# Another order of the layers' slots, of the layers' end and of the last tile's down rows

## The reference

```python
# block 1: 64 features (DIM), 4 layers, inner width 256
h = x @ Win.T + bin
for each layer:
    y = silu(layernorm(h, l1w, l1b))
    y = sconv(y)          # y[t] = Re(sum over s<=t of p**(t-s) y[s] + last * p**(t+1))
    h = h + y * scl
    y = layernorm(h, l2w, l2b)
    h = h + silu(y @ W1.T + b1) @ W2.T + b2
x = norm(x + layernorm(h, lnl_w, lnl_b) @ Wout.T + bout)
# block 2: weights are looked up in a codebook of 8192 rows of 8 numbers
Wg, Wu, Wd = codebook[idx_gate], codebook[idx_up], codebook[idx_down]   # 1376x512, 1376x512, 512x1376
x = norm(x + (silu(x @ Wg.T) * (x @ Wu.T)) @ Wd.T)
```

## Time and profile before

| | |
|---|---|
| median of three runs | 1266.31 us |
| the profiled execution, its own time | 1264.5 us |
| its span, first to last instruction | 1262.5 us |
| PE busy | 1188.8 us (94%) |
| DVE busy | 1011.6 us (80%) |
| POOL busy | 929.9 us (74%) |
| ACT busy | 261.7 us (21%) |
| mean granted clock of PE | 0.982 of full speed |

### The profile page before, as it was taken

How to read it: one execution, slowest core, us unless ns; L and a number is a source line. 1 busy time by engine, 2 the same in 40 slices (tenths; PEclk the granted TensorE clock), 3 DMA queues, 4 the chain that set the end, 5 groups by cost and what they waited for, 6 DMA issues and landing times.

```text
span 1262.5 us, 16835 instructions
## 1 busy us (share of the span) xinstructions
PE 1188.8 (94%) x5595; PEld 839.3 (66%) x5595; DVE 1011.6 (80%) x2194; ACT 261.7 (21%) x395; POOL 929.9 (74%) x895
## 2 busy tenths in 40 slices
PE   6857998889999999999999999999999999999998
PEld 4533444346777777777777777777777777778876
DVE  3998898878997778888777888778888778888845
ACT  2325777772000000000000000000000000000024
POOL 6777777777777777777777777777777777777710
PEclk8968999989999999999999999999999999999999
DMA  9331211102433223433223433333433333334303
GB/s 202 64 68 37 45 37 39 27 4 53 105 92 87 65 71 80 95 82 92 65 69 79 89 85 81 65 70 86 93 85 87 67 70 79 94 72 88 60 2 133
DMA packets 96971, 93.57 MB, mean 74 GB/s; under 512 B 53549, under 2 KB 57909, under 8 KB 96886
## 3 DMA queue, kind: packets, MB, share of 16 engines
q1 hardware_dynamic: 64692, 83.86, 23.0%
q0 software_dynamic: 28160, 3.66, 8.5%
q10 hardware_dynamic: 4034, 4.98, 1.4%
HBM read 87.53 MB, written 4.90 MB: 73 GB/s over the span
## 4 chain that ended last, share of the span: by engine, by line
POOL 73%; issue 21%; PE 4%; DMA 1%; DVE 0%; ACT 0%; POOLq 0%; SPq 0%; DVEq 0%
POOL stage_down L400 57%; POOL stage_up L389 16%; PE bank L652 2%; PE cand L652 2%; DMA work<-in_L_ffn_idx_up 0%; DMA stage_down<-in_L_ffn_codebook,idx_down 0%; ACT x L505 0%; POOLq L160 0%; DVE chosen L1229 0%; DVE x L1033 0%; PE bank L924 0%; SPq L315 0%; DVE idx_low L1091 0%; DVE idx_low L1092 0%; DVE shift L1239 0%
## 5 line engine op out<-in xcount | busy, mean ns | idle before, releaser
L400 POOL DMA_INDIRECT stage_down<-in_L_ffn_codebook,idx_down x688 | 722.3, 1050 | 209.7 <-issue 209.1
L652 PE MATMUL cand<-one_hot,book 128*128 128x512 f32 (+1 forms) x2432 | 622.7, 398 | 19.0 <-DVE one_hot L1057 19.0
L1057 DVE TENSOR_SCALAR one_hot<-bc,low_of 128x512 fp32r<-128x512 uint16 (+1 forms) x1216 | 512.8, 482 | 99.0 <-PE cand L652 97.3
L652 PEld LDWEIGHTS cand<-one_hot,book 128*128 128x128 f32 x2432 | 449.7, 189 | 187.2 <-DVE one_hot L1057 51.8
L389 POOL DMA_INDIRECT stage_up<-in_L_ffn_codebook,idx_up x192 | 205.6, 1071 | 63.8 <-issue 58.2
L652 PE MATMUL bank<-x1t_hi,w 128*128 128x512 f32 (+1 forms) x704 | 239.1, 396 | 0.0
L1075 DVE SCALAR_TENSOR_TENSOR chosen<-bc,high_of,cand 128x512 f32<-128x512 uint16 (+1 forms) x304 | 220.2, 724 | 21.1 <-PE bank L652 17.9
L652 PEld LDWEIGHTS bank<-x1t_hi,w 128*128 128x128 f32 (+1 forms) x704 | 130.3, 185 | 31.4 <-issue 2.1
L652 PE MATMUL bank<-x1t_lo,w 128*128 128x512 f32 (+1 forms) x352 | 137.7, 391 | 0.0
L598 ACT ACTIVATE prod<-bank 128x512 f32<-128x512 f32 (+1 forms) x44 | 26.3, 599 | 389.4 <-PE bank L652 389.4
L605 ACT ACTIVATE act_hi<-prod 128x512 fp32r<-128x512 f32 x40 | 25.3, 633 | 342.5 <-DVE prod L1033 342.5
(11 more groups left out here) (181 smaller groups left out, 751.8 us busy)
## 6 DMA issues: line engine op xcount, KB each, us to landing
bc<-index_parts SPq DMA_DIRECT2D x272, 256.0 KB, 3.3
stage_down<-in_L_ffn_codebook,idx_down POOLq DMA_INDIRECT x688, 2.7
bc<-index_parts_rest SPq DMA_DIRECT2D x32, 192.0 KB, 3.1
x<-in_L_attn_x ACTq DMA_DIRECT2D x4, 1024.0 KB, 9.8
out_x<-x SPq DMA_DIRECT2D x16, 256.0 KB, 2.0
stage_up<-in_L_ffn_codebook,idx_up POOLq DMA_INDIRECT x192
index_parts<-parts_t SPq DMA_DIRECT2D x20, 32.0 KB, 2.0
w_in<-in_L_attn_W ACTq DMA_DIRECT2D x2, 256.0 KB
```

The lines of the kernel that those rows point to most:

```text
L400: pool.indirect_dma_start(stage_down[k % RING][:, q, j * CS:(j + 1) * CS], None, a["L0_ffn_codebook"], bass.IndirectOffsetOnAxis(ap=idx_do ...
L652: return pe.matmul(dst, lhs, rhs, start=start, stop=stop)
L1057: done = v.tensor_scalar(one_hot[quad % 2][:, q, 0:nw], bc[quad % BCS][:, 0:nw], low_of[:, q:q + 1], None, ALU.is_equal)
```

## The change

In the slots, PE's `mixed(t - 1)` moves from ahead of `variance1(t)` to behind `spread(t - 2)`; DVE's `add_mixed(t - 1)` moves from the slot's start to behind `choose` of the first quad, and `add_back` ahead of `norm2`; ACT's `silus` moves ahead of `square2`. The damped d gets a second buffer. In the layers' end, ACT makes roots together and silus together, so that one pair of table loads falls away, and PE's and DVE's steps are put in an order that suits it. In the tail, the last tile's down rows are turned after chunk 1 instead of chunk 0, and with them `down` and `out_chunk` come one chunk later; another two table loads fall away there.

```diff
-            work = at("work", [P, 13, C])
+            work = at("work", [P, 14, C])
+        d = [work[:, n, :] for n in (6, 13)]
@@ ACT, slot t
+                if t >= 2:
+                    silus(t - 2)
                 if t:
                     square2(t - 1)
-                if t >= 2:
-                    silus(t - 2)
                 square1(t + 1)
@@ ACT, layers' end
+            def tile_root(n):
+                act.wait_ge(s["aggregated"], n + 1)
+                root(rstd[:, n:n + 1], mv[:, n, 1:2]).then_inc(s["rstd_made"], 1)
             square2(ITEMS - 1)
+            root2(ITEMS - 1)
+            tile_root(0)
             silus(ITEMS - 2)
+            silus(ITEMS - 1)
             square1(ITEMS + 1)
-            root1(ITEMS + 1)
-            root2(ITEMS - 1)
-            for n in range(NT + 2):
+            for n in range(1, NT + 2):
                 if n == 2:
-                    silus(ITEMS - 1)
                     square1(ITEMS + 2)
+                if n == 3:
+                    root1(ITEMS + 2)
...
+                if n == 1:
+                    root1(ITEMS + 1)
@@ PE
             def mixed(i):
                 pe.wait_ge(s["damped"], i + 1)
-                if i >= 3:
-                    pe.wait_ge(s["h_made"], i - 2)
-                mm(bank[0][:, :], mix[:, i // NC, :], d).then_inc(s["mixed"], 1)
+                if i:
+                    pe.wait_ge(s["h_mid"], i)
+                if i >= 2:
+                    pe.wait_ge(s["h_made"], min(ITEMS - NC + 1, i - 1))
+                mm(bank[0][:, :], mix[:, i // NC, :], d[i % 2]).then_inc(s["mixed"], 1)
...
-                if t:
-                    mixed(t - 1)
                 variance1(t)
...
                 if t >= 2:
                     spread(t - 2)
+                if t:
+                    mixed(t - 1)
@@ PE, layers' end
             back(ITEMS - 3)
+            variance2(ITEMS - 1)
             project(0)
             spread(ITEMS - 2)
             project(1)
+            spread(ITEMS - 1)
+            back(ITEMS - 2)
             variance1(ITEMS + 1)
-            variance2(ITEMS - 1)
-            back(ITEMS - 2)
@@ PE, tail
-            for c in range(NC + 1):
+            for c in range(NC + 2):
                 if c < NC:
                     hidden(FULL, REST, c, 0, 1)
-                if c == 0:
+                if c == 1:
                     turn_down(FULL, REST)
-                else:
-                    for t in range((c - 1) * TPC, c * TPC):
+                if c >= 2:
+                    for t in range((c - 2) * TPC, (c - 1) * TPC):
@@ DVE, slot t
-                if t:
-                    add_mixed(t - 1)
                 one_hots(quads[0] + 1)
...
+                if t >= 3:
+                    add_back(t - 3)
                 if t >= 2:
                     norm2(t - 2)
-                if t >= 3:
-                    add_back(t - 3)
...
+                if t >= 2:
+                    v.wait_ge(s["mixed"], t - 1)
+                tt(d[t % 2], g, tab[:, l, :], ALU.mult).then_inc(s["damped"], 1)
+                choose(quads[0])
                 if t:
-                    v.wait_ge(s["mixed"], t)
-                tt(d, g, tab[:, l, :], ALU.mult).then_inc(s["damped"], 1)
-                choose(quads[0])
+                    add_mixed(t - 1)
```

More of the change, by code:

```diff
@@ L235, in build @@
             centre = at("centre", [P, P])
-        sq1, rs1, xn, y, u, g, d = (work[:, n, :] for n in range(7))
+        sq1, rs1, xn, y, u, g = (work[:, n, :] for n in range(6))
+        d = [work[:, n, :] for n in (6, 13)]
         sq2 = [work[:, 7 + b, :] for b in range(2)]
@@ L566, in _ @@
             square2(ITEMS - 1)
+            root2(ITEMS - 1)
+            tile_root(0)
             silus(ITEMS - 2)
+            silus(ITEMS - 1)
             square1(ITEMS + 1)
-            root1(ITEMS + 1)
-            root2(ITEMS - 1)
-            for n in range(NT + 2):
+            for n in range(1, NT + 2):
                 if n == 2:
-                    silus(ITEMS - 1)
                     square1(ITEMS + 2)
+                if n == 3:
+                    root1(ITEMS + 2)
                 if n == 4:
-                    root1(ITEMS + 2)
-                if n == 5:
                     square1(ITEMS + 3)
-                if n == 7:
+                if n == 6:
                     root1(ITEMS + 3)
@@ L584, in _ @@
                     normalize(n - 1, n, "x1_made")
+                if n == 1:
+                    root1(ITEMS + 1)
                 if n < NT:
-                    act.wait_ge(s["aggregated"], n + 1)
-                    root(rstd[:, n:n + 1], mv[:, n, 1:2]).then_inc(s["rstd_made"], 1)
+                    tile_root(n)
             def down_hi(k, n):
@@ L638, in _ @@
                 product_hi(FULL, REST, c)
-                if c == 0:
+                if c == 1:
                     down_hi(FULL, REST)
-                if c >= 2:
-                    out_chunk(c - 2)
+                if c >= 3:
+                    out_chunk(c - 3)
+            out_chunk(NC - 3)
             out_chunk(NC - 2)
@@ L866, in variance2 @@
                     pe.wait_ge(s["state_kept"], t // NC * (NC - 1) + t % NC)
-                if i:
+                if i == ITEMS - 1:
+                    pe.wait_ge(s["rs2_made"], i)
+                elif i:
                     pe.wait_ge(s["ff_made"], i)
@@ L872, in back @@
                 pe.wait_ge(s["ff_made"], i + 1)
-                pe.wait_ge(s["h_mid"], min(ITEMS, i + 3))
+                pe.wait_ge(s["h_mid"], i + 2 if i < ITEMS - 3 else ITEMS)
                 if i:
@@ L881, in spread @@
                 pe.wait_ge(s["normed2"], i + 1)
-                pe.wait_ge(s["rs1_made"], min(ITEMS + 2, i + 3))
-                pe.wait_ge(s["rs2_made"], i + 1)
+                if i == ITEMS - 1:
+                    pe.wait_ge(s["ff_made"], i)
+                pe.wait_ge(s["rs1_made"], min(ITEMS + 1, i + 3))
+                pe.wait_ge(s["rs2_made"], i + 1 if i < ITEMS - 2 else ITEMS)
                 for k in range(FK):
@@ L958, in _ @@
             project(1)
+            spread(ITEMS - 1)
+            back(ITEMS - 2)
             variance1(ITEMS + 1)
-            variance2(ITEMS - 1)
-            back(ITEMS - 2)
             for n in range(1, NT + 1):
+                if n == 2:
+                    back(ITEMS - 1)
                 if n == 3:
                     variance1(ITEMS + 2)
-                    back(ITEMS - 1)
-                if n == 6:
+                if n == 5:
                     variance1(ITEMS + 3)
@@ L969, in _ @@
                     project(n + 1)
-                if n == 1:
-                    spread(ITEMS - 1)
                 if n in AHEAD_STEPS:
@@ L1325, in _ @@
                     norm2(ITEMS - 1)
+                if n == 2:
                     add_back(ITEMS - 2)
-                if n == 2:
                     norm_last(1)
-                if n == 4:
+                if n == 3:
                     add_back(ITEMS - 1)
@@ L1401, in _ @@
                     product_lo(FULL, REST, c)
-                if c == 0:
+                if c == 1:
                     down_lo(FULL, REST)
+                if c >= 3:
+                    make_shift((c - 3) * TPC, TPC, NT + c - 2)
                 if c >= 2:
-                    make_shift((c - 2) * TPC, TPC, NT + c - 1)
-                if c:
-                    for t in range((c - 1) * TPC, c * TPC):
+                    for t in range((c - 2) * TPC, (c - 1) * TPC):
                         add_down(last_pair, t, (bank[2][:, :], cand[0][:, :], cand[1][:, :], cand[2][:, :]))
```

6 lines of the change are left out of this document (3 added, 3 removed).

## The result

The changed kernel takes 1297.04 us, the median of four runs (1294.10 to 1299.75), against 1266.82 for the kernel before: a ratio of 1.0245, 95% interval 1.0208 to 1.0283. It is slower, as forecast, but by 30 us where the sum said 18: inside the range of 8 in 10 (1268 to 1300) and outside the forecast's own (1277 to 1292). The profiled execution took 1294.88 us, its span is 1293.1 and PE's mean granted clock 0.969 instead of 0.982. One of the ten executions of f2_end_warm, a kernel further down, took 2626 us, and its ratio leaves that one out.

What follows compares the result with a forecast made beforehand. PE bounds the main stage, a cycle of waits the slots before it; 12.3 + 2 + 3 + 1 - 0.3 = +18.0 us on the profiled 1264.5 gives 1282.5, forecast 1284 us against the median, own range 1277 to 1292, 8 in 10: 1268 to 1300.

Steps and rivals of the forecast that it cites:

- square2's 1.4 us: Sign, slots: square2's wait for DVE's h addition, about 1.4 us each, becomes ACT's largest wait there.
- root1(16): Sign, start of the layers' end: this root comes 14 to 18 us later than before.
- 240 to 291: Sign, stretch of the layers' end ahead of the main stage: keeps its length within 4 us.
- Cycle of the slot: Slots 4 to 15: cycle of waits grows from 8.71 to 9.92 us, +12.3 us in all with two-group slots and picks.
- Slots 0 to 3: First four slots: 41 us instead of 38.9, +2 (0 to +4).
- PE's clock in the slots: Slots: PE's pauses of about 2.7 us drop its clock; four slots of 0.8, +3 us (bounds 0 and +10).
- the fall at 116: Earlier trace: PE busy 1.36 of 3.6 us up to 116.0, then granted clock 0.50 at 118 to 120.
- Layers' end: End of the layers: one pair of table loads saved, new waits; -1 at 2.4 GHz, about +4 at 1.2 GHz, taken +1 us.
- Tail: Last tile: PE's 0.34 us wait for the last gather goes, -0.3 us.
- Addition not last: Rival, slots: add_mixed done before silus ends, cycle 8.44 us, total 1256 us; chance 0.08.
- Hidden: Rival: longer cycle right, but early, two-group and last slots give back as much, about 1266 us; chance 0.08.
- The clock's rival: Every slot's pause drops PE to 1.2 GHz, 17.6 us instead of 3, end +4: 1302 us; chance 0.12.

Runs made afterwards that it cites:

- f2_end_warm: Changed kernel with slots in the order of before, new end and tail kept, 18 extra matmuls in the end's pauses: 1267.7 us.
- e2: Changed kernel with its layers' end put back into the order of before, new slots and tail kept: 1293.2 us.
- e5: Changed kernel with add_mixed ahead of choose on DVE, nothing else, on the slower chip: ratio 1.0061 to 1.0104 to the kernel before.
- f1_three: Changed kernel with norm2 ahead of add_back, add_mixed ahead of choose and square1 ahead of square2; new end and tail kept: 1273.4 us.
- e3: Changed kernel with norm2 ahead of add_back again on DVE, nothing else: 1294.9 us.
- e1: Changed kernel with the slots of all three engines in their order of before; new end and tail kept: 1271.8 us.
- e11: f1_three with the layers' end of before as well: 1272.4 us.

## Why the prediction was right, and where it was too small

Of its signs, the period, square2's 1.4 us, the vanished wait for mixed, PE's pause and the length of the main stage came. Three did not: root1(16) came 23.7 us later and not 14 to 18, 240 to 291 grew by 7.4 us and not by at most 4, and ACT's largest wait was silus'.

- **Cycle of the slot: right.** 9.92 forecast; 9.91 and 9.93 measured, square2's wait 1.37 (1.4 forecast), PE's pause 2.83 (2.7). Twelve slots at full clock come to about 123 (e2's slope) or 13.2 us more than before (the full slots' mean), against 122.3 and +12.3. e5 and f1_three show the cause: with add_mixed ahead of choose the slot is 9.26 us, and with square1 ahead of square2 as well (and norm2 ahead of add_back) 8.74, as forecast from the same steps. Twelve slots at 9.92 were not seen in one run: slots 13 and 14, at 1.00 and 0.99, took 10.55 and 10.51.
- **Slots 0 to 3: right**, +2.3 against +2.
- **PE's clock in the slots: mechanism right, size wrong.** "I take four slots of 0.8, +3" measured 8.8, near the upper bound of 10. Six of twelve slots had a fall, 1.5 us each and not 0.8. Two things were missed. A slow back, variances and spread follow each other in the slot, so the slot pays more than one of them; and add_back ahead of norm2, which the sum costed at nothing, puts norm2 behind the slow back as well (some 4 of the 8.8, by e3's one profile). The row chosen against the bound, 0.54 of 2 us busy at 144 to 146 with the clock left at 1.00, was from a kernel whose slots pause less. The Trainium skill ("TensorE: Matmul & The Clock Gate", section "HAM oscillation — how this bites in real kernels") says that repeated pauses throttle the clock again and again; the slots here agree with it (0.92 against 1.00), though PE's pauses, 3.2 us at most, are shorter than those of the page's example. It and the fall at 116 together should have weighed more than that one row.
- **Layers' end: the step that failed.** "+1", with a bound of +4; measured +7.4. Up to tile 4 it is +3.6: the walk was right for 2.4 GHz (22.42 in f2 against 22.9), but its "-1" set this against a 23.7 of before that was measured at 0.86. At that clock the new order is 2.3 us longer (f1, and 2.4 in e1), and a longer fall (0.81) adds 1.3. Why it is longer is argued and not shown: tile 0's normalisation now stands behind silus(15), and silus(15) waits 4.89 us for spread(15) and back(14). No run has the first part of before's end at full clock, so its "-1" can't be told. And "From tile 4 on both go by DVE's 2 us a tile" was wrong at 1.2 GHz, where PE sets this part: 31.95 at 0.79 instead of 28.17, +3.8. After, the addition for tile 6 waits, PE and then DVE:

```profile
294.88 2.07 PE L659 MATMUL cand<-woutt,work 65*128 65x512 f32 x2
```

```profile
296.99 0.69 DVE L1046 TENSOR_TENSOR x<-x,cand 128x512 f32<-128x512 f32 x1 [2.47 <-PE cand L659]
```

  The projection takes 2.07 us behind a variance of 2.07 (each 1.12 at full clock), and DVE is idle for 2.47. The saved table loads are real (ACT's busy time in the end falls from 37.97 to 35.76 us); the end is longer all the same.
- **Tail: right as far as can be told**, -0.5 for main stage and tail against -0.3, from one profile of before. The gap of the earlier trace rows is gone: `turn_down`'s first row has no idle before it. POOL waited 20.2 us once for PE's unit, and it cost nothing, as PE is later still.

```profile
POOL stage_up L390 <- PE bank L659: 23.1, 2, 20.2
```

- **Rivals.** "Addition not last" and "Hidden" did not come. The clock's rival (17.6 in the slots, end +4: 1302) is half true, and the measured 1297 lies nearer to it than to the forecast's 1284. 8.8 in the slots and 5.1 of the 7.4 in the end go with a lower clock than before, and the other 2.3 are the new order at before's clock. Together they are 16 us where the sum had 4, which is nearly the whole miss of 12 us. That the direction was right owes nothing to luck, as the cycle alone gives 13 of the 30 us; that the time fell into the wide range owes something to it.

What stays open is what makes a fall come in one execution and not in the next of the same instructions.

## What to carry to other kernels

Where several engines hand work round in a cycle, price the exchange of two neighbours by who waits behind the later one: here an addition behind four steps of DVE, with two squares, a table load and the roots queued behind it, made each slot 1.2 us longer, and three exchanges of neighbours gave back 24 us, falls of the clock included. A change that lengthens PE's pauses must be priced at both clocks for every later step, those that another engine seems to set included, and the measured part of before that it is compared with must be read with its clock. Filling pauses with extra matmuls moved the falls more than it removed them, and delayed the real work.

## What the runs showed of the hardware

- One fall of PE's clock costs this kernel about 3 us (14.34 against 11.37, 13.96 against 10.74 for slots with the same instructions), and the times of e11's runs follow the clock: 1264.5 at 0.981, 1275.1 at 0.972.
- Time at 1.2 GHz costs about 0.4 us per us in slots that PE does not fill (e2 against after 0.42; e11 against f1 4.5 us for 12.0, both good to some 0.1), and 0.3 in the end's second part (3.8 us for 13.4).
- In the slots PE was never idle for more than 3.2 us at a time by the waits, and the clock fell in six of twelve.
- On one chip of three every kernel took 1.7 times as long (2167 against 1267 us), in stalls of tens of us, while single slots kept their length to 0.01 us (8.73 against 8.74).
- A table load took 1.28 us and the next function began 0.02 us behind it (167.10 and 168.40).
